# A macaron block (FFN, attention, FFN) on one core: value bias moved into the projection's bias, values copied by ScalarE, constant key rows written by DMA

## The reference, cut to what matters

```python
x = x + 0.5 * ffn(layernorm(x))        # W_r, W_k, W_v, mu_r, mu_k
x = x + attention(layernorm(x))        # below
x = x + 0.5 * ffn(layernorm(x))

# attention: 16 heads of 16 channels, causal
qkv = x @ W_qkv + b_qkv                # 256 -> 768
q, k, v = split(qkv); q, k = rope(q), rope(k)
att = softmax(mask(q @ k.T / 4))
y = att @ v                            # each row of att sums to 1
return y @ W_proj + b_proj
```

## Time and profile before

| | |
|---|---|
| Median of 3 runs | 3276.06 us |
| Profiled execution, own time | 3273.49 us |
| Its span in the trace | 3271.6 us |
| Mean granted TensorE clock | 0.982 of full |
| PE busy | 3063.4 us |
| DVE busy | 2523.8 us |
| ACT busy | 2150.6 us |
| POOL busy | 1502.2 us |

### The profile page before, as it was taken

One profiled execution on the slowest core, in us unless ns is written; L12 is line 12 of the kernel. 1 busy time (PEld: TensorE's weight loads), 2 busy tenths in 40 slices (PEclk: granted clock), 3 DMA queues, 4 the chain that ended last, 5 costly groups with the idle time before them and its releaser, 6 DMA issues.

```text
span 3271.6 us, 57505 instructions
## 1 busy us (share of the span) xinstructions
PE 3063.4 (94%) x18368; PEld 1644.3 (50%) x18368; DVE 2523.8 (77%) x8449; ACT 2150.6 (66%) x4737; POOL 1502.2 (46%) x2135
## 2 busy tenths in 40 slices
PE   5689999999999999999999999999999999999997
PEld 3434555555555555555555555555555555555434
DVE  3678788887878878878887888878787887888862
ACT  3266667676666667667676666766667666766663
POOL 5343454444544544444554544444444454454322
PEclk9799999999999999999999999999999999999997
DMA  2344344334434434434424433443443433443421
GB/s 86 52 66 76 62 84 85 73 76 74 89 61 94 76 71 85 76 78 74 92 62 74 96 63 83 85 74 76 73 89 60 95 72 70 87 75 71 78 54 33
DMA packets 201142, 245.35 MB, mean 75 GB/s; under 512 B 67845, under 2 KB 102025, under 8 KB 200841
## 3 DMA queue, kind: packets, MB, share of 16 engines
q1 hardware_dynamic: 200840, 241.69, 37.1%
HBM read 53.35 MB, written 51.38 MB: 32 GB/s over the span
## 4 chain that ended last, share of the span: by engine, by line
PE 79%; DVE 9%; ACT 6%; issue 3%; POOL 2%; DMA 1%; SPq 1%; POOLq 0%; DVEq 0%; ACTq 0%
PE ps_y L597 16%; PE ps_s L575 15%; PE ps_m L582 12%; PE ps_d L648 7%; PE ps_d L645 7%; PE ps_d L642 7%; PE ps_d L654 6%; DVE ps_m L777 5%; PE ps_d L632 3%; PE ps_d L604 3%; ACT pt_sb L683 3%; PE ps_d L658 2%; ACT qb_sb L733 1%; ACT xt_sb L692 1%; DVE mx_sb L777 1%
## 5 line engine op out<-in xcount | busy, mean ns | idle before, releaser
L777 DVE CUSTOM_DVE_ANT_0 ps_m<-ps_m,mask_sb 128x512 f32<-128x512 f32 (+3 forms) x3072 | 1694.0, 567 | 584.0 <-PE ps_m L582 570.5
L683 ACT ACTIVATE pt_sb<-ps_s 128x512 f32<-128x512 f32 (+3 forms) x3072 | 1468.1, 493 | 952.7 <-PE ps_s L575 933.3
L575 PE MATMUL ps_s<-qr_sb,kr_sb 99*128 99x512 bf16 (+3 forms) x3072 | 1006.3, 332 | 37.3 <-ACT pt_sb L683 27.5
L582 PE MATMUL ps_m<-kr_sb,qr_sb 96*128 96x512 bf16 (+3 forms) x3072 | 996.9, 328 | 29.9 <-DVE mx_sb L777 14.1
L902 POOL TENSOR_SCALAR_AFFINE_SELECT pt_sb<-pt_sb 128x512 f32<-128x512 f32 x512 | 338.3, 661 | 943.0 <-ACT pt_sb L683 940.0
L575 PEld LDWEIGHTS ps_s<-qr_sb,kr_sb 99*128 99x128 bf16 x3072 | 298.0, 98 | 819.7 <-ACT pt_sb L683 345.2
L597 PE MATMUL ps_y<-pt_sb,v_sb 128*32 128x512 f32 (+3 forms) x6144 | 660.5, 502 | 0.0
L777 DVE DVE_READ_ACCUMULATOR2_ANT mx_sb<- 128x1 f32 x3072 | 432.1, 141 | 0.0
L582 PEld LDWEIGHTS ps_m<-kr_sb,qr_sb 96*128 96x128 bf16 x3072 | 297.8, 97 | 152.9 <-DVE mx_sb L777 42.9
L654 PE MATMUL ps_d<-axn_sb,wqk_sb 128*128 128x256 f32 x1024 | 304.7, 397 | 7.8 <-DVE x_sb L848 2.6
L642 PE MATMUL ps_d<-ka_sb,wk_sb 128*128 128x256 f32 x1024 | 300.5, 390 | 7.0 <-DVE ka_sb L801 4.0
(11 more groups left out here) (74 smaller groups left out, 3227.7 us busy)
## 6 DMA issues: line engine op xcount, KB each, us to landing
kr_sb<-part_sb SPq DMA_DIRECT2D x384, 128.0 KB, 4.5
qr_sb<-part_sb SPq DMA_DIRECT2D x384, 128.0 KB, 4.8
sw_sb<-qb_sb SPq DMA_DIRECT2D x512, 64.0 KB, 2.0
y_way<-yt_sb SPq DMA_DIRECT2D x128, 256.0 KB, 3.0
x_sb<-x SPq DMA_DIRECT2D x64, 256.0 KB, 2.9
yn_sb<-y_way SPq DMA_DIRECT2D x64, 256.0 KB
den_sb<-r_way SPq DMA_DIRECT2D x64, 256.0 KB
out<-x_sb SPq DMA_DIRECT2D x64, 256.0 KB, 2.2
```

What stands on the lines that cost most here:

```text
L575: eng.matmul(ps_s[:, slot % NS, 0:width], kr_sb[0:KR + NP, n % RS, j, kb * P:(kb + 1) * P], qr_sb[0:KR + NP, n % RS, j, q0:q0 + width], st ...
L582: eng.matmul(ps_m[:, u % NM, 0:width], qr_sb[0:KR, n % RS, j, i * P:(i + 1) * P], kr_sb[0:KR, n % RS, j, piece * QC:piece * QC + width], s ...
L683: eng.activation(pt_sb[:, tick % 2, j, 0:width], ps_s[:, slot % NS, 0:width], ACT.Exp, scale=SCALE).then_inc(exped, 1)
L777: eng.tensor_tensor_reduce(ps_m[:, u % NM, 0:width], ps_m[:, u % NM, 0:width], mask_sb[:, m0:m0 + width], 1.0, -3e38, ALU.add, ALU.max, mx ...
```

## The change

The value bias is no longer added to the values. Once, near the start, PE multiplies it with the projection's matrix (`b_P`, two products of 1x256), DVE adds the result to the projection's bias (`b_add`), and POOL splits the sum as before. The values are moved from `ps_d` to `v_sb` by one copy of 128x512 on ACT (`a_vc`) in place of DVE's two additions. The ones in `kr_sb` are written by three DMA transfers from `one_sb` in place of POOL's three memsets, and only the score products wait for them. ACT has no wait at its start any more, DVE waits for POOL's constants before its first reduction, and PE waits for the 11 settings that are left.

```diff
-        if name == "a_bv":
+        if name == "a_vc":
             early = max(early, (i // NCH - 1) * BSLOTS + PV_AT + 1)
...
-                s("DVE", "a_bv", i, 0.67, t + 100, ("a_V", i, 1))
+                s("ACT", "a_vc", i, 0.5, t + 100, ("a_V", i, 1))
...
-        s("POOL", "b_split", 0, 1.5, 1)
+        s("PE", "b_P", 0, 2, 1)
+        s("DVE", "b_add", 0, 0.5, 1, ("b_P", 0, 1))
+        s("POOL", "b_split", 0, 1.5, 1, ("b_add", 0, 2))
...
-              "a_V": "a_bv", "p_P": "xp", "m_T": "m_copy"}
+              "a_V": "a_vc", "p_P": "xp", "m_T": "m_copy", "b_P": "b_add"}
...
-        N_SET_POOL = 11 + RS
+        N_SET_POOL = 11
...
-                             (bv_sb[:, :], b_v.broadcast_to([P, C])), (cos_sb[:, :], rope_c), (sin_sb[:, :], rope_s),
+                             (bv_sb[:, :], b_v), (cos_sb[:, :], rope_c), (sin_sb[:, :], rope_s),
...
+            sp.wait_ge(set_pool, 1)
+            for r in range(RS):
+                eng.dma_start(kr_sb[KR:KR + NP, r, :, :].rearrange("o j (i q) -> o (j i) q", q=P),
+                              one_sb[0:NP, :].rearrange("p (o n) -> p o n", o=1).broadcast_to([NP, G * TT, P])).then_inc(ones_in, 16)
...
                 pe.wait_ge(*mrows_ready(n))
+                pe.wait_ge(ones_in, 16 * RS)
...
+                if name == "b_P":
+                    pe.wait_ge(consts, N_CONST)
+                    mm = eng.matmul(ps[0:1, 0:C], bv_sb[:, u:u + 1], wp_sb[:, u, :], start=(u == 0), stop=(u == CC - 1))
+                    if u == CC - 1:
+                        mm.then_inc(made[d], 1)
+                    return
...
             act = Once(eng)
-            act.wait_ge(consts_ffn, N_FFN)
-            act.wait_ge(set_pool, N_SET_POOL)
...
+                elif name == "a_vc":
+                    b, c = divmod(i, NCH)
+                    d = plan.bank["a_V", i]
+                    dst = v_sb[:, b % 2, c * CT:(c + 1) * CT, 0:H * VW].rearrange("p t (h w) -> p t h w", w=VW)[:, :, :, 0:HS]
+                    act.wait_ge(*made_by("a_V", i))
+                    act.wait_ge(pved, (b - 1) * NG * NTK)
+                    eng.activation(dst, ps_d[:, d, :].rearrange("p (t h d) -> p t h d", t=CT, d=HS), ACT.Copy).then_inc(taken[d], 1)
...
-            dve.wait_ge(set_pool, N_SET_POOL)
 
             def take_max(u):
                 n, i, j, piece, width, diagonal = piece_of(u)
                 m0 = QC + P - width if diagonal else 0
+                dve.wait_ge(set_pool, N_SET_POOL)
...
-                elif name == "a_bv":
-                    b, c = divmod(i, NCH)
-                    d = plan.bank["a_V", i]
-                    dve.wait_ge(*made_by("a_V", i))
-                    dve.wait_ge(pved, (b - 1) * NG * NTK)
-                    for t in range(CT):
-                        dst = v_sb[:, b % 2, c * CT + t, 0:H * VW].rearrange("p (h w) -> p h w", w=VW)[:, :, 0:HS]
-                        v = eng.tensor_tensor(dst, ps_d[:, d, halves(t)].rearrange("p (h d) -> p h d", d=HS),
-                                              bv_sb[:, :].rearrange("p (h d) -> p h d", d=HS), ALU.add)
-                    v.then_inc(taken[d], 1)
+                elif name == "b_add":
+                    dve.wait_ge(*made_by("b_P", 0))
+                    eng.tensor_tensor(bp_sb[:, 0, :], bp_sb[:, 0, :], product_of("b_P", 0)[0:1, 0:C],
+                                      ALU.add).then_inc(taken[plan.bank["b_P", 0]], 1)
...
-            for r in range(RS):
-                pool.wait_ge(set_pool, N_SET_POOL - RS + r)
-                eng.memset(kr_sb[KR:KR + NP, r, :, :], 1.0).then_inc(set_pool, 1)
             pool.wait_ge(set_pool, N_SET_POOL)
```

More of the change, by code:

```diff
@@ L295, in place @@
             for c in range(NCH):
-                assert self.slots["a_bv", b * NCH + c] < b * BSLOTS
+                assert self.slots["a_vc", b * NCH + c] < b * BSLOTS
 class Once:
@@ L367, in macaron @@
         bqk_sb = sb("bqk_sb", [P, 4])
-        bv_sb = sb("bv_sb", [P, C])
+        bv_sb = sb("bv_sb", [P, CC])
         cos_sb = sb("cos_sb", [P, T])
@@ L385, in macaron @@
         scaled = sem("scaled")
+        ones_in = sem("ones_in")
         x_in = [[sem(f"x_in{r}_{c}") for c in range(NCH)] for r in range(XR)]
@@ L957, in dense @@
                     rest = bp_sb[:, 1, :]
-                    pool.wait_ge(consts, N_CONST)
+                    pool.wait_ge(*taken_from("b_P", 0))
                     eng.tensor_copy(hi, bp_sb[:, 0, :]).then_inc(bias_split, 1)
@@ L1000 @@
     w_v = np.asarray(L0_attn_W_qkv).reshape(C, H, 3, HS)[:, :, 2].reshape(C, C)
-    b_v = np.asarray(L0_attn_b_qkv).reshape(H, 3, HS)[:, 2].reshape(1, C)
+    b_v = np.asarray(L0_attn_b_qkv).reshape(H, 3, HS)[:, 2].reshape(CC, P).T
     rope_c, rope_s = rope_tables()
```

## The result

The changed kernel takes 3239.82 us, the median of 4 runs (3238.39 to 3241.48), against 3275.72 for the kernel before; the ratio is 0.9892, 95% interval [0.9875, 0.9909]. Forecast were 3240 us and 35 us less. Its profiled execution took 3241.48 us.

The account below looks back on a forecast made before the run. PE's stream bounds the kernel, busy 3063.4 of 3271.6 us. Terms -9.7 + 1.5 - 29.2 - 3.3 + 1.1 + 4.4 = -35.2 us on 3273.49, plus 2.6 for the median, gave 3240.9, stated as 3240; range 3230 to 3252.

Parts of the forecast that it names:

- The start: Before PE runs steadily: 7.0 + 1.3 + 1.4 = 9.7 us less, bounds 5 and 13.
- the bias: `b_P` adds two products to PE and a transpose stands two slots behind `b_add`: 1.5 us more, bounds 0.5 and 3.
- The memsets and the table load: At the start: without POOL's memsets statistics begin 7.0 us earlier; ACT's table load runs early, 1.3 us less.
- rival B: At the start, PE's slow clock or late loads take half back: 3245 us, inside the forecast's range, no separate chance.
- the product that waited 1.4 us: An FFN product at 110.8 us, waiting for a value addition behind DVE's first maxima: 1.4 us less.
- The 26 waits: Transposes waiting for DVE's value addition, 39.4 us in all: 29.2 us less, bounds 12 and 39.4.
- the first place: The transpose at 1020.82 us, of the kind waiting 1.12 us: 0.8 us gained each, counted 14 times.
- the second place: The transpose at 1069.14 us, of the kind waiting 1.98 us: 1.5 us gained each, counted 12 times.
- The new wait for `f_u`: In 13 batches a value product stands two slots behind `f_u` on DVE: 0.3 us each, 4.4 us more, bounds 0 and 20.
- The copy on ACT: 64 value copies of 602 ns; scores waiting for exponentials behind them cost PE 1.1 us, bounds 0 and 38.
- Rival D: ACT's copy holds back the exponential and PE stops with two score buffers: slower, up to 3318 us; chance 0.04.
- DVE's relief: DVE loses 47.8 us of work; an eighth of the 28 us left gives 3.3 us less, bounds 0 and 10.

Follow-up runs that it names:

- the values part alone: The changed kernel with POOL's memsets and the waits at the head as in the kernel before: 3247.31 us, ratio 0.9908.
- The start part alone: The kernel before with ones by DMA, no waits at ACT's head and DVE's wait moved; value bias and additions kept: 3269.35 us, ratio 0.9973.
- The old order with ACT's copy: The changed kernel with the value copy planned as a DVE step, so PE has the order of before, but executed by ACT: 3235.77 us, ratio 0.9872.
- the second copy: The changed kernel with another ACT copy of 128x512 to a spare tile before each value copy: 3252.95 us, ratio 0.9919.
- the new order with the old engine: The changed kernel with its order of all other steps, but DVE executes the value copy in ACT's slot: 3314.72 us, ratio 1.0108.
- the last kernel: The changed kernel with ACT's copy in the order planned for DVE, three slots after `f_u` and `b_add`, first statistics before the weights: 3254.68 us, ratio 0.9926.

## Why the prediction was right

The mechanism held in both parts; the total of 35 us is met better than its terms.

- **The start**: forecast 9.7 us less 1.5 for the bias, arrived 6.8. The memsets and the table load gave 7.8 of 8.3 us at the first transpose. Then PE's products ran at half pace for longer: eight products took 3.41 us at 24.40 in place of 1.99, and eight more 3.65 at 37.45 in place of 1.97, so that the first product for maxima stands 4.0 us earlier only (104.33 for 108.34). This is the forecast's rival B, which I had put at half of the start's gain. The rest of the 6.8 came back between 105 and 190 us, where DVE has less to do: the product that waited 1.4 us went at once, and the values part alone gains 2.1 us there, with the first transpose and the first product for maxima where they were. But how much of a lead survives to 104 us differs from trace to trace. The start part alone brought all but 0.2 of its 8.4 us there (100.16 for 108.34). Among the kernels with the changed kernel's start, 6.8, 9.3 and 7.6 us arrive at 190 us with ACT copying, 2.5 and 6.0 with DVE copying, and 8.3 with the additions of before. So that the changed kernel lost half at the start is seen in one execution, and is not shown to be the change's doing.
- **The 26 waits**: forecast 0.8 and 1.5 us of gain; by the landmarks around them 1.1 at the first place (0.6 with the new wait for `f_u`) and 1.2 at the second. The one was too low by as much as the other was too high, so their sum of 29.2 us holds (14 x 1.1 + 12 x 1.2 = 29.8) by a chance of the two errors. In the times of the kernel before the first transpose stands at 1021.48; I had 1021.45. At the second place DVE's statistics now stand together in front of the reduction, and the product for maxima waits 0.25 us. The forecast worked these gains out through the new order, with the transpose behind `m_copy`. The old order with ACT's copy gains 0.3 us more in a batch, so the reader's engine was needed and the new order was not.
- **The new wait for `f_u`**: 0.47 us in place of 0.3, 6.1 us in place of 4.4.
- **The copy on ACT**: 600 ns, 602 forecast; 1.4 us more of waits for exponentials, 1.1 forecast. Rival D is refuted by the second copy.
- **DVE's relief**: 3.3 us forecast. In a steady batch nothing of it shows (1.1 + 1.2 - 0.5 is 1.8, which the landmarks have); it shows in the start.
- **Missed**: the clock. The long waits had cost about 1.5 us more each time that the clock fell at one, 3 us in the profiled execution; the start part alone, with the same waits, met four falls. The changed kernel no longer has them, but lost 2.2 us between 190 and 371 us, with a fall at 294. The forecast knew of neither.

In sum by landmarks: 6.8 at 190, -2.2 to 371, 23.2 in 13 batches, 3.1 of clock, 0.9 after: 31.8 at the last, and 32.0 between the two profiled executions. The medians give 35.9. The difference lies between executions, and the forecast's hit within 1 us is luck by as much.

What the prediction did not see is how far the credit belongs to the distance between a reader and the next user of its buffer. It named DVE's backlog as the cause and took the move to ACT for the cure. A slot more after DVE's readers does as much as the values part (0.9906 and 0.9908) and takes no work from DVE; with both, and the first statistics ahead of the weights, the kernel is at 3207 us.

## What to carry to other kernels

Where two engines in a fixed order hand a buffer back and forth, look at what stands in the reader's queue in front of the read, not at the read's length: 2 x 0.415 us of addition on a loaded DVE held PE for up to 1.98 us, one of 0.60 on ACT for 0.47 on average and 0.7 at most. Try the cheap cure first, one place more between the reader and the next user, and try it again after the move. Once an order is written by a planner, measure every combination: the new order with the old engine was 1.1% slower than the kernel before, and the best edits put together in another order, with one slot left out, kept 0.7% where their best combination has 2.2%.

## What the runs showed of the hardware

A wait of PE of one to two and a half microseconds can cost more than itself. The granted clock went from 1.00 to 0.50 for 3.4 us at the end of such a wait, which cost about 1.5 us more. It did not do so at each: at two of the twelve waits of 1.98 us in the kernel before and at four in the kernel with the start part alone, at 11 of 12 waits of 2.46 us, and at four waits of 1.24 us in the last kernel. At 294 us of the changed kernel it fell at a wait of 0.83 us that followed one of 0.59.

At the start the products' pace shows the low level also where the recorded clock does not: eight products took 3.41 us at 24.40, with 1.00 recorded from 24 to 28 us, and 3.65 at 37.45, where 0.50 is recorded for 3.4 us from 37.54 on. How far that pace takes an earlier start back differs between executions. A first transpose 7.8 us earlier brought 4.0 us at the first product for maxima in the changed kernel; one 8.4 us earlier brought 8.2 with the start part alone.
